# A recommendation tower on one core: the last tile's field pairs in two parts, and first layers one place ahead

## The chip, the cores and the metric

The kernel runs on one core of one Trainium2 chip. The metric is the device time of the program in microseconds (us), as the median of its runs. The profile comes from one execution of its own.

## What is computed

For each of 2048 samples the reference takes 50 rows of 16 numbers, one from each of 50 tables, forms the dot product of every pair of different rows, and runs a small tower of three layers over these 1225 products and 16 dense numbers.

```python
e = jnp.stack([tbl_0[ids[:, 0]], ..., tbl_49[ids[:, 49]]], axis=1)       # 2048 x 50 x 16
gram = jnp.einsum('bid,bjd->bij', e, e)
z = gram[:, I, J]                                                      # the 1225 pairs with i < j
h = jnp.concatenate([z, dense_ctx], axis=1)                            # 1241 columns
h = jnp.maximum(h @ W_top1 + b_top1, 0.0)                              # 512
h = jnp.maximum(h @ W_top2 + b_top2, 0.0)                              # 256
y = h @ W_top3
```

Of the tables 29 have 1000 or 1250 rows (`SMALL`), seven have 12500 and fourteen have 125000.

## The kernel before

**Tiles.** The samples are 16 tiles of 128 (`NTILES`), four to a chunk (`TPC`); `FINAL` is 12, the first tile of the last chunk, and `LAST` is 15. A product of two fp32 numbers is kept exact enough by splitting each into a high and a low fp16 part.

**Where the rows come from.** The 29 small tables and two of 12500 rows (`MED`) lie on the chip: VectorE (DVE) writes one-hot columns (`compare`), TensorE (PE) multiplies them with the table (`look_up`), chunk by chunk and one chunk ahead. ScalarE (ACT) moves the picked rows into `split` (`move`). The other 19 fields (`REST`, `NR` = 19) are gathered from memory by GpSimd (POOL), one indirect DMA for each field and tile (`gathers`, line 448). In the last chunk nothing is looked up any more.

**A tile's way.** When all gathers of a tile have landed, DVE splits them (`split_rows`, lines 576, 580, 589) and transposes all 50 rows in blocks of 32 (`turn`, line 604). PE forms the 50 by 50 products of two samples at a time, a matmul of 32 rows and 100 columns for each of four row groups (`dots`; in the last chunk `half_dots`, line 841, eight halves of 32 matmuls over two row groups and two sample pairs, so 16 matmuls each by the trace's count). ACT and DVE copy each half out of PSUM into `gram` (`copy_half`, lines 1018 and 644); half h waits until half h-2 has been copied. Then nine rectangles (`PIECES`) of `gram` for each of two sides are moved by DMA into `z`, where the pairs i < j lie densely on 125 partitions and 11 columns (`pack`, line 383 on the queue of SyncE, SP). ACT makes the high part of `z` (`split_products`, line 1077), DVE the low part (line 552). The first layer is 33 matmuls of 512 columns (`first_part`, line 881), 22 with the high part and 11 with the low one. The 512 results go through ACT (line 1102), are transposed (`mlp(T, TURN_STEP)`, line 933), copied (line 1106), and multiplied with the second layer's weights (`mlp(T, L2_STEP)`, line 938). DVE makes the last layer (`score`, lines 704 and 706).

**The order.** Every engine runs a list that is written out by hand. Within the last chunk PE has: halves of tile 12 with the first layer of 10 between them; halves of 13; first layers of 11 and 12 with the rest of 11; halves of 14; rest of 12; first layer and rest of 13; halves of 15, from the third on with two matmuls of tile 14's first layer between them (line 902); the rest of 14 (lines 902, 909, 933, 938); and tile 15 (`last_mlp`, lines 854, 858, 866, 874). DVE, ACT and SP have lists to match. All of tile 15's pack follows its last half: SP issues six of side 0, ACT six of side 1 (line 1096), POOL the six small corners (line 472).

**The last tile's gathers.** DVE takes tile 15 in two steps (`last_rows`): the first nine gathered fields with all looked-up ones, then the last ten (lines 620, 624, 625, 636). The halves of tile 15 wait for both.

```python
def half_dots(T, h):
    if h == 0:
        pe.wait_ge(turned_ready, 2 * T + (2 if T < LAST else 4))
```

Of the kernel before, what the change touches and what calls it, by code (L numbers as in the profile page):

```python
# [15 lines left out]
NF = 50  # L16
ND = 16
TILE = 128
TPC = 4
# [25 lines left out]
FIELD = SMALL[:EVEN] + MED + SMALL[EVEN:] + REST  # L45
# [22 lines left out]
JS = EVEN // 2  # L68
JM = NM // 2
# [7 lines left out]
TOP = 5  # L77
PIECES = []
_p = 0
for _g in range(4):  # L80
    _r = ST * _g + TOP + 1
    PIECES.append((_r, NF - _r, ST * _g, ST, _p, 0))
    _p += NF - _r
TOP_P = _p
for _g in range(5):
    PIECES.append((ST * _g + 1, TOP, ST * _g, TOP, TOP_P + TOP * (_g // 2), TOP * (_g % 2)))
DENSE_P = TOP_P + 3 * TOP
DENSE_R = 2
# [66 lines left out]
BIG_PIECES, CORNERS = PIECES[:6], PIECES[6:]  # L155
LAST = NTILES - 1
FINAL = (NCH - 1) * TPC
LAST_KS = (range(0, 6), range(6, ST))
LAST_J = (JS + JM, JS + JM + 5, JJ)
LAST_FIELDS = 2 * (LAST_J[1] - LAST_J[0]) - 1  # L160
HALVES = 2 * EVACS
FILL_FROM, FILL = 2, 2
# [11 lines left out]
ONE_K = ST - 1  # L174
L1_BETWEEN = 6
# [9 lines left out]
def build(nc, small, med, big, ids_small, ids_med, ids_sample, ids_big, dense, w1, w2, b2, w3, y):  # L185
    ctx = ExitStack()
    with ctx:
# [64 lines left out]
        hid_last = gram_ps[:, 0, :]  # L252
# [52 lines left out]
        corners_in = sem("corners_in")  # L305
# [32 lines left out]

        block = ctx.enter_context(nc.Block())
# [5 lines left out]
        def _(sp):  # L345
# [20 lines left out]
            def pack(T, sides=range(TWO), pieces=PIECES):  # L366
# [7 lines left out]

                if T < FINAL:
                    sp.wait_ge(gram_copied, TWO * EVACS * (T + 1))
                else:
                    sp.wait_ge(half_by_act, halves_of(T))
                    sp.wait_ge(half_by_dve, halves_of(T))
                for a in sides:  # L380
                    for piece in pieces:
                        out, src = piece_of(piece, T, a)
                        sp.dma_start(out, src).then_inc(packed[T % 2], 16)  # L383

# [38 lines left out]
            pack(NTILES - 1, (0,), BIG_PIECES)  # L423

        @block.gpsimd
        def _(pool):
# [14 lines left out]
            def gathers(T):  # L441
# [3 lines left out]
                for f in range(NR):  # L445
                    landed = gathered[T % TPC] if T < LAST or f < LAST_FIELDS else gathered_last
                    pace(T, f)
# [21 lines left out]
            for a in range(TWO):  # L469
                for piece in CORNERS:  # L470
                    out, src = piece_of(piece, LAST, a)
                    pool.dma_start(out, src).then_inc(corners_in, 16)

        @block.vector
        def _(dve):
# [89 lines left out]
            def rows_by_parity(T):  # L565

                t = T % TPC
                return [(emb[:, t, 1 - a:NR:2, :], split[:, t, JS + JM + 1 - a:JJ, 0, :, a],
                         split[:, t, JS + JM + 1 - a:JJ, 1, :, a]) for a in range(2)]

            def split_rows(T):
# [10 lines left out]
                known = JS + JM  # L582
# [683 lines left out]
```

## Time and profile before

| what | value |
|---|---|
| runs | 453.38, 453.18 and 456.85 us, median 453.38 us |
| profiled execution, its own time | 453.39 us |
| its span, first to last instruction | 451.3 us |
| mean granted TensorE clock | 0.89 of full speed |
| PE / PE weight loads / DVE / ACT / POOL busy | 76% / 55% / 66% / 44% / 71% |

```profile
POOL 5788777777777777787777777778777777776020
PEclk9978659978679997989999969699998895988999
```

Each digit of these two lines is a fortieth of the span, 11.3 us, in tenths. POOL gathers at an even pace until slice 37 and is then nearly idle. The clock line holds the TensorE clock that was granted: it is full or half in any moment, so a digit between is a mixture.

### The profile page before, as it was taken

How to read it: one execution, taken by the hardware profiler on the slowest of the kernel's cores; microseconds unless marked ns; L12 is line 12 of the kernel's file. 1: busy time of each engine (PE TensorE's matmuls, PEld its weight loads, DVE VectorE, ACT ScalarE, POOL GpSimd, SP SyncE). 2: the span in 40 equal slices, each digit the busy share in tenths (PEclk: the TensorE clock that was granted, in tenths of full speed). 3: DMA queues.
4: the chain of work that ended last, by engine and by line, in shares of the span. 5: the costliest groups of instructions: out<-in, count | busy, mean ns of one | idle time of the engine just before them, and what ended most of it. 6: DMA issues, size and time to landing. Idle time of an engine off the chain costs nothing.

```text
span 451.3 us, 13158 instructions
## 1 busy us (share of the span) xinstructions
PE 342.9 (76%) x5633; PEld 247.4 (55%) x5633; DVE 295.8 (66%) x606; ACT 198.8 (44%) x288; POOL 322.7 (71%) x318
## 2 busy tenths in 40 slices
PE   0568167566488979979989699798895948989886
PEld 0567067565366657666666476656653525454543
DVE  2599899999357579758576687566715437165551
ACT  2335712246235774455457653445487324140511
POOL 5788777777777777787777777778777777776020
PEclk9978659978679997989999969699998895988999
DMA  6994503423321344243213433111121222212020
GB/s 161 407 367 142 173 7 101 118 77 86 82 44 39 104 115 94 63 136 88 47 32 103 115 95 65 36 43 36 40 53 24 66 50 50 48 15 61 5 61 1
DMA packets 24638, 38.92 MB, mean 86 GB/s; under 512 B 8532, under 2 KB 15876, under 8 KB 24452
## 3 DMA queue, kind: packets, MB, share of 16 engines
q1 hardware_dynamic: 14166, 35.04, 24.0%
q0 software_dynamic: 9920, 2.55, 6.6%
q8 instruction: 44, 0.72, 0.7%
q10 hardware_dynamic: 494, 0.49, 0.3%
q14 instruction: 14, 0.11, 0.1%
HBM read 26.98 MB, written 0.14 MB: 60 GB/s over the span
## 4 chain that ended last, share of the span: by engine, by line
PE 34%; DVE 18%; ACT 13%; SPq 11%; issue 10%; DMA 8%; POOL 5%; another core or an unknown queue 0%; DVEq 0%; ACTq 0%; POOLq 0%
PE hid_ps L881 12%; SPq L383 11%; DVE onehot L490 9%; PE look_ps L803 8%; ACT gram L1010 6%; POOL emb L448 5%; DMA ids_bc<-ids_dram 5%; PE mid_ps L938 5%; PE gram_ps L820 3%; ACT z_both L1077 2%; DVE turned L604 2%; PE gram_ps L841 2%; ACT looked L1047 2%; DMA z_both<-gram 2%; DVE w_sb L672 1%
## 5 line engine op out<-in xcount | busy, mean ns | idle before, releaser
L448 POOL DMA_INDIRECT emb<-tbl,gidx x304 | 318.9, 1049 | 95.7 <-issue 88.4
L881 PE MATMUL hid_ps<-w_sb,z_both 127*128 127x512 f16 x462 | 112.3, 386 | 0.0
L803 PE MATMUL look_ps<-parts,onehot 125*128 125x64 f16 x1836 | 75.0, 203 | 44.5 <-DVE onehot L490 29.9
L490 DVE TENSOR_SCALAR onehot<-ids_bc,rows 125x2048 f16<-125x2048 f16 (+1 forms) x144 | 92.2, 690 | 19.2 <-PE look_ps L803 14.7
L803 PEld LDWEIGHTS look_ps<-parts,onehot 125*128 125x128 f16 x1836 | 69.5, 105 | 56.2 <-issue 20.8
L1010 ACT ACTIVATE gram<-gram_ps 50x784 f32<-50x784 f32 x96 | 78.2, 815 | 29.6 <-PE gram_ps L820 26.7
L803 PE MATMUL look_ps<-parts_med,onehot 125*128 125x128 f16 x800 | 57.1, 233 | 14.4 <-DVE onehot L490 13.8
L881 PEld LDWEIGHTS hid_ps<-w_sb,z_both 127*128 127x128 f16 x462 | 41.5, 99 | 46.1 <-issue 3.3
L803 PEld LDWEIGHTS look_ps<-parts_med,onehot 125*128 125x128 f16 x800 | 53.1, 105 | 20.6 <-DVE parts_med L663 13.9
L490 DVE TENSOR_SCALAR onehot<-ids_bc,rows_med 125x1024 f16<-125x1024 f16 x100 | 45.8, 495 | 28.2 <-PE look_ps L803 24.4
L1047 ACT ACTIVATE looked<-look_ps 128x1024 f16<-128x1024 f32 (+1 forms) x28 | 26.7, 954 | 67.0 <-PE look_ps L803 66.6
L820 PE MATMUL gram_ps<-turned 32*128 32x100 f16 x1536 | 28.6, 216 | 25.4 <-ACT gram L1010 23.1
L604 DVE STREAM_TRANSPOSE turned<-split 128x800 uint32<-128x800 uint32 x30 | 46.6, 1625 | 0.5
L938 PE MATMUL mid_ps<-w_sb,h_turned 128*128 128x256 f32 x120 | 37.8, 469 | 2.8 <-ACT h_turned L1106 2.1
L820 PEld LDWEIGHTS gram_ps<-turned 32*128 32x128 f16 x1536 | 20.8, 99 | 31.3 <-ACT gram L1010 25.9
L552 DVE SCALAR_TENSOR_TENSOR z_both<-z_both 127x704 f16<-127x704 f32 x30 | 25.3, 884 | 12.3 <-ACT z_both L1077 12.3
L1102 ACT ACTIVATE h<-hid_ps 128x512 f32<-128x512 f32 x14 | 8.4, 597 | 56.4 <-PE hid_ps L881 51.8
L938 PEld LDWEIGHTS mid_ps<-w_sb,h_turned 128*128 128x128 f32 x120 | 27.2, 238 | 8.5 <-ACT h_turned L1106 2.9
L1077 ACT ACTIVATE z_both<-z_both 127x1408 f16<-127x1408 f32 x15 | 20.6, 1371 | 11.1 <-DMA z_both<-gram 11.1
L644 DVE TENSOR_SCALAR gram<-gram_ps 50x392 f32<-50x392 f32 x32 | 17.4, 568 | 11.7 <-PE gram_ps L841 11.6
L1018 ACT ACTIVATE gram<-gram_ps 50x392 f32<-50x392 f32 x32 | 15.3, 490 | 21.4 <-PE gram_ps L841 21.2
L841 PE MATMUL gram_ps<-turned 32*128 32x100 f16 x512 | 17.4, 223 | 8.8 <-DVE turned L604 5.2
(74 smaller groups left out, 221.7 us busy)
## 6 DMA issues: line engine op xcount, KB each, us to landing
ids_bc<-ids_dram SPq DMA_DIRECT2D x28, 512.0 KB
emb<-tbl,gidx POOLq DMA_INDIRECT x304
z_both<-gram SPq DMA_DIRECT2D x31, 121.0 KB
z_both<-w SPq DMA_DIRECT2D x1, 2816.0 KB
z_both<-gram SPq DMA_DIRECT2D x31, 90.8 KB
z_both<-gram SPq DMA_DIRECT2D x152, 6.2 KB
z_both<-gram SPq DMA_DIRECT2D x31, 60.5 KB
gram<-small SPq DMA_DIRECT2D x2, 512.0 KB, 5.1
```

The costliest lines, as they stand in the source:

```text
L383: sp.dma_start(out, src).then_inc(packed[T % 2], 16)
L448: pool.indirect_dma_start(emb[:, T % TPC, f, :], None, big[f], bass.IndirectOffsetOnAxis(ap=gidx[:, T, f:f + 1], axis=0)).then_inc(landed, 16)
L490: nc.vector.tensor_scalar(onehot[0:TP, s % RING, 0:cnt, :], ids_bc[0:TP, o % IDS_BUFS, 0:cnt, :], row, None, ALU.is_equal).then_inc(onehot ...
L604: nc.vector.transpose(out, src[:, :, w0:w0 + WORDS]).then_inc(turned_ready, 1)
L803: last = nc.tensor.matmul(bank[:, half, at:at + width], onehot[0:TP, at_ring, i, t * TILE:(t + 1) * TILE], moving.rearrange("p i s d -> p ...
L820: last = nc.tensor.matmul(gram_ps[:, r, i * TWO * NF:(i + 1) * TWO * NF], turned[p, T % 2, b:b + TWO, :].rearrange("p a m -> p (a m)"), bu ...
L841: last = nc.tensor.matmul(gram_ps[:, r, i * TWO * NF:(i + 1) * TWO * NF], turned[p, T % 2, b:b + TWO, :].rearrange("p a m -> p (a m)"), bu ...
L881: return nc.tensor.matmul(hid_ps[:, :], z_parts[0:KP, T % 2, x, k, :], w1_sb[0:KP, k, w, :], start=(i == 0), stop=(i == L1_MM - 1))
L938: last = nc.tensor.matmul(out_ps, h1_turned[:, n, :], w2_sb[:, n, :], start=(n == 0), stop=(n == N1 - 1))
L1010: nc.scalar.activation(out, src, ACT.Copy, scale=1.0 / (SCALE * SCALE)).then_inc(gram_copied, 1)
L1047: nc.scalar.activation(out, src, ACT.Copy).then_inc(looked_ready, 1)
L1077: nc.scalar.activation(halves(T, 0), products(T), ACT.Copy, scale=ZSCALE).then_inc(z_hi, 1)
```

## The change

**Order of the fields.** `FIELD` has the 19 gathered fields first (0 to 18), then the odd small one, the other small ones and the two medium ones. The rectangles of `gram` are cut anew: two for the columns 0 to 9 (`LATE_PIECES`), seven for the columns from 10 on (`EARLY_PIECES`), nine in all as before. They hold as many numbers, but in 243 rows of 1280 or 1536 bytes a side, where it was 135 rows of 2816 or 1280 bytes.

**The last tile.** Its gathers run from field 10 to 18 and then 0 to 9. After the first nine, DVE turns fields 10 to 49, PE forms the halves with 80 columns instead of 100, and ACT and DVE copy them (`early_evacuation`, 312 elements instead of 392). Then DVE turns fields 0 to 9, PE forms all pairs with these in `late_dots`, 128 matmuls of 20 columns, ACT and DVE copy them in four pieces each (`late_evacuation`, 160 elements), and the two late pieces a side are packed. The first layer of tile 15 begins with the six columns of `z` that the early pieces fill, and the rest of tile 14 stands between its parts.

**The last chunk.** The first layers of 11, 12 and 13 stand one place ahead: before the halves of 13, after them, and before the halves of 14. The transposes and second layers of 11 and 13 stand between the halves of 13 and 14. The two matmuls of tile 14's first layer between the halves of 15 are gone: it stands as a whole after the late products. In tiles 13 and 14 ACT issues six of side 1's nine pieces, and SP twelve of the eighteen; in tile 15 POOL issues side 1's seven early ones.

```diff
-FIELD = SMALL[:EVEN] + MED + SMALL[EVEN:] + REST
+FIELD = REST + SMALL[EVEN:] + SMALL[:EVEN] + MED
...
+LATE = 10
+LATE_K = 5
+PIECES = [(1, NF - 1, 0, LATE_K, 0, 0), (LATE_K + 1, NF - LATE_K - 1, LATE_K, LATE_K, NF - 1, 0)]
 _p = 0
+for _c in range(LATE, 34, ST - LATE_K):
+    PIECES.append((_c + 1, NF - _c - 1, _c, ST - LATE_K, _p, LATE_K))
+    _p += NF - _c - 1
+_p = sum(nr for _, nr, c, *_ in PIECES if c < LATE)
+for _c in range(34, NF - 1, LATE_K):
+    PIECES.append((_c + 1, NF - _c - 1, _c, LATE_K, _p, 0))
+    _p += NF - _c - 1
+LATE_PIECES, EARLY_PIECES = PIECES[:2], PIECES[2:]
+SP_PIECES, ACT_PIECES = PIECES[:3], PIECES[3:]
...
+LAST_KS = (range(LATE_K, ST), range(LATE_K))
...
 # SyncE
-                for a in sides:
-                    for piece in pieces:
+                for a in range(TWO):
+                    for piece in (PIECES if a == 0 or T <= FINAL else SP_PIECES):
...
+            def pack_last():
+                begin_pack(LAST)
+                sp.wait_ge(half_by_act, halves_of(LAST))
+                sp.wait_ge(half_by_dve, halves_of(LAST))
+                for piece in EARLY_PIECES: ...
+                sp.wait_ge(late_by_act, Q)
+                for piece in LATE_PIECES: ...
...
 # VectorE, the order in the last chunk
             for h in range(HALVES):
                 copy_half(FINAL, h)
+            split_products(FINAL - 1)
+            score(FINAL - 2)
             split_rows(FINAL + 1)
             turn(FINAL + 1)
-            split_products(FINAL - 1)
             for h in range(HALVES):
                 copy_half(FINAL + 1, h)
-            score(FINAL - 2)
+            score(FINAL - 1)
             split_products(FINAL)
-            score(FINAL - 1)
+            split_products(LAST - 2)
             split_rows(LAST - 1)
             turn(LAST - 1)
+            score(FINAL)
             for h in range(HALVES):
                 copy_half(LAST - 1, h)
-            split_products(LAST - 2)
+            score(LAST - 2)
             last_rows(0)
-            score(LAST - 3)
-            last_rows(1)
             for h in range(HALVES):
                 copy_half(LAST, h)
+            last_rows(1)
             split_products(LAST - 1)
-            score(LAST - 2)
+            for r in range(Q):
+                copy_late(r)
+            split_last(0)
             activate(LAST - 1)
+            split_last(1)
             copy_turned(LAST - 1, N1, mlp_copied)
...
 # TensorE
+            def late_dots():
+                T = LAST
+                pe.wait_ge(turned_ready, 2 * T + 4)
+                pe.wait_ge(half_by_act, halves_of(T))
+                pe.wait_ge(half_by_dve, halves_of(T))
+                for h in range(2):
+                    for b in range(0, SPQ, TWO):
+                        for buf in (turned, turned2):
+                            for r in range(Q // 2 * h, Q // 2 * (h + 1)):
+                                p = slice(32 * r, 32 * r + 32)
+                                last = nc.tensor.matmul(
+                                    gram_ps[:, r, b * LATE:(b + TWO) * LATE],
+                                    turned[p, T % 2, b:b + TWO, :].rearrange("p a m -> p (a m)"),
+                                    buf[p, T % 2, b:b + TWO, 0:LATE], start=(buf is turned), stop=(buf is turned2))
+                    last.then_inc(late_done, 1)
...
+            first_part(FINAL - 1, 0, L1_MM)
             for h in range(HALVES):
                 half_dots(FINAL + 1, h)
-            first_part(FINAL - 1, 0, L1_MM)
-            mlp(FINAL - 1, TURN_STEP)
-            first_part(FINAL, 0, L1_BETWEEN)
-            mlp(FINAL - 1, L2_STEP)
-            first_part(FINAL, L1_BETWEEN, L1_MM)
+                if h == TURN_AT:
+                    mlp(FINAL - 1, TURN_STEP)
+                if h == L2_AT:
+                    mlp(FINAL - 1, L2_STEP)
+            high_part(FINAL)
+            low_part(FINAL)
+            mlp(FINAL, TURN_STEP)
+            mlp(FINAL, L2_STEP)
+            high_part(LAST - 2)
+            low_part(LAST - 2)
             for h in range(HALVES):
                 half_dots(LAST - 1, h)
-            mlp(FINAL, TURN_STEP)
-            mlp(FINAL, L2_STEP)
-            first_part(LAST - 2, 0, L1_MM)
-            mlp(LAST - 2, TURN_STEP)
-            mlp(LAST - 2, L2_STEP)
-            fill = 0
+                if h == TURN_AT:
+                    mlp(LAST - 2, TURN_STEP)
+                if h == L2_AT:
+                    mlp(LAST - 2, L2_STEP)
             for h in range(HALVES):
                 half_dots(LAST, h)
-                if h >= FILL_FROM:
-                    high_part(LAST - 1, fill, fill + FILL)
-                    fill += FILL
-            high_part(LAST - 1, fill, 2 * ST)
+            late_dots()
+            high_part(LAST - 1)
             low_part(LAST - 1)
+            last_high(0)
+            last_low(0)
             mlp(LAST - 1, TURN_STEP)
+            last_high(1)
             mlp(LAST - 1, L2_STEP)
+            last_low(1)
             last_mlp()
...
 # ScalarE
+            copy_mlp(FINAL - 1, FEED - 1)
             for h in range(HALVES):
                 copy_half(FINAL + 1, h)
+                if h == TURN_AT:
+                    copy_mlp(FINAL - 1, TURN_STEP + 1)
             split_products(FINAL)
-            copy_mlp(FINAL - 1, FEED - 1)
-            copy_mlp(FINAL - 1, TURN_STEP + 1)
+            pack(FINAL + 1)
             copy_mlp(FINAL, FEED - 1)
-            for h in range(HALVES):
-                copy_half(LAST - 1, h)
             copy_mlp(FINAL, TURN_STEP + 1)
             split_products(LAST - 2)
             copy_mlp(LAST - 2, FEED - 1)
-            copy_mlp(LAST - 2, TURN_STEP + 1)
-            split_products(LAST - 1)
+            for h in range(HALVES):
+                copy_half(LAST - 1, h)
+                if h == TURN_AT:
+                    copy_mlp(LAST - 2, TURN_STEP + 1)
+            pack(LAST - 1)
             for h in range(HALVES):
                 copy_half(LAST, h)
-            pack(LAST, BIG_PIECES)
+            split_products(LAST - 1)
+            for r in range(Q):
+                copy_late(r)
+            pack_late()
```

`high_part(T)` and `low_part(T)` are now the 22 and the 11 matmuls of a first layer; the first waits for the high part of `z` alone.

## Rows read from the trace of the kernel before

**Rows 1.** Chain that ended last, from tile 13's last gather: start us, us, what.

```profile
366.11 2.40 DMA emb<-tbl,gidx
...
379.68 8.94 PE hid_ps L881 x33
...
443.31 1.09 PE gram_ps L858 x5
...
449.18 0.27 ACT h L1194
```

**Rows 2.** Timeline, gathers: start us, us, engine, line; in brackets the idle time before.

```profile
402.24 0.95 POOL L448 DMA_INDIRECT emb<-tbl,gidx  x1 [0.30 <-issue]
...
415.04 0.95 POOL L448 DMA_INDIRECT emb<-tbl,gidx  x1 [0.30 <-issue]
...
417.30 0.32 DVE L620 TENSOR_SCALAR split<-emb 128x80 f16<-128x80 f32 x2 [4.65 <-DMA emb<-tbl,gidx]
```

**Rows 3.** Timeline, what ends second layer 10 and starts first layer 11.

```profile
365.42 1.37 ACT L1077 ACTIVATE z_both<-z_both 127x1408 f16<-127x1408 f32 x1
365.57 1.99 PE L938 MATMUL mid_ps<-w_sb,h_turned 128*128 128x256 f32 x8 [0.69 <-ACT h_turned L1106]
...
372.56 1.67 DVE L552 SCALAR_TENSOR_TENSOR z_both<-z_both 127x704 f16<-127x704 f32 x2
```

**Rows 4.** Timeline, halves of products: tile 13 at half clock, tile 14 at full.

```profile
374.98 1.33 PE L841 MATMUL gram_ps<-turned 32*128 32x100 f16 x32 [1.05 <-DVE gram L644]
...
376.58 1.33 PE L841 MATMUL gram_ps<-turned 32*128 32x100 f16 x32 [0.28 <-ACT gram L1018]
...
400.15 1.01 PE L841 MATMUL gram_ps<-turned 32*128 32x100 f16 x32 [0.63 <-DVE gram L644]
400.72 1.05 DVE L644 TENSOR_SCALAR gram<-gram_ps 50x392 f32<-50x392 f32 x2 [0.23 <-PE gram_ps L841]
```

**Rows 5.** Timeline, weight loads of products: over four row groups, then over two.

```profile
346.86 0.64 PEld L820 LDWEIGHTS gram_ps<-turned 32*128 32x128 f16 x32 [3.92 <-ACT gram L1010]
...
351.35 0.63 PEld L841 LDWEIGHTS gram_ps<-turned 32*128 32x128 f16 x16 [0.65 <-issue]
...
423.40 0.38 PEld L841 LDWEIGHTS gram_ps<-turned 32*128 32x128 f16 x16 [0.42 <-issue]
```

**Rows 6.** Windows of one microsecond: PE, PEld, DVE, ACT, POOL busy, PEclk, DMA, GB/s.

```profile
373.00:374.00 1.00, 0.93 (x32) 0.70 (x26) 1.00 (x2) 0.30 (x1) 0.69 (x2) 0.50 0.28 65
...
382.00:383.00 1.00, 1.00 (x4) 0.30 (x3) 1.00 (x2) 0.00 (x0) 1.00 (x1) 0.50 0.51 147
...
402.00:403.00 1.00, 0.73 (x29) 0.61 (x30) 1.00 (x2) 0.97 (x2) 0.76 (x1) 1.00 0.15 24
...
404.00:405.00 1.00, 0.82 (x4) 0.41 (x2) 0.38 (x1) 0.45 (x2) 0.70 (x2) 0.50 0.04 3
...
410.00:411.00 1.00, 1.00 (x5) 0.40 (x4) 1.00 (x2) 0.00 (x0) 0.95 (x1) 0.80 0.11 15
```

**Rows 7.** Timeline, the rest of a tile: transposes, second layer at half clock, score.

```profile
417.80 0.63 PE L933 MATMUL mid_ps<-identity,h 128*128 128x128 f32 x4 [0.78 <-ACT h L1102]
418.47 0.60 ACT L1106 ACTIVATE h_turned<-mid_ps 128x512 f32<-128x512 f32 x1 [0.81 <-PE mid_ps L933]
...
405.50 3.78 PE L938 MATMUL mid_ps<-w_sb,h_turned 128*128 128x256 f32 x8 [0.69 <-ACT h_turned L1106]
```

**Rows 8.** Timeline, last tile's turning on DVE, and the packs' issue on each queue.

```profile
409.23 2.50 DVE L636 STREAM_TRANSPOSE turned<-split 128x640 uint32<-128x640 uint32 x2
...
404.46 13.44 SPq L383 DMA_DIRECT2D z_both<-gram  x18
...
428.63 5.60 ACTq L1096 DMA_DIRECT2D z_both<-gram  x6
429.17 3.06 POOL L472 DMA_DIRECT2D z_both<-gram  x6 [13.19 <-DVE gram L644]
...
435.49 1.47 ACT L1087 ACTIVATE z_both<-z_both 127x768 f16<-127x768 f32 x2 [7.05 <-DMA z_both<-gram]
```

More of the change, by code:

```diff
@@ L364, in load_sample_ids, with begin_pack @@
                 sp.dma_start(odd[:, n % 2, :, :], ids_sample[n, :, :, :]).then_inc(sample_in[n % 2], 16)
-            def pack(T, sides=range(TWO), pieces=PIECES):
+            def begin_pack(T):
                 if T >= 2:
@@ L373, in pack @@
                              dense[:, T, :, :]).then_inc(dense_in[T % 2], 16)
+            def pack(T):
+                begin_pack(T)
                 if T < FINAL:
@@ L422, in _ @@
                     pack(T - 1)
-            pack(NTILES - 1, (0,), BIG_PIECES)
+            pack_last()
         @block.gpsimd
@@ L444, in gathers @@
                     pool.wait_ge(emb_read, T + 1 - TPC)
-                for f in range(NR):
-                    landed = gathered[T % TPC] if T < LAST or f < LAST_FIELDS else gathered_last
-                    pace(T, f)
+                for i in range(NR):
+                    f = (LATE + i) % NR
+                    landed = gathered[T % TPC] if T < LAST or f >= LATE else gathered_last
+                    pace(T, i)
                     pool.indirect_dma_start(
@@ L468, in _ @@
             pool.wait_ge(half_by_dve, halves_of(LAST))
[L469 to L472, printed above, removed]
+            for piece in EARLY_PIECES:
+                out, src = piece_of(piece, LAST, 1)
+                pool.dma_start(out, src).then_inc(early_by_pool, 16)
         @block.vector
@@ L567, in rows_by_parity @@
                 t = T % TPC
-                return [(emb[:, t, 1 - a:NR:2, :], split[:, t, JS + JM + 1 - a:JJ, 0, :, a],
-                         split[:, t, JS + JM + 1 - a:JJ, 1, :, a]) for a in range(2)]
+                return [(emb[:, t, a:NR:2, :], split[:, t, 0:JR - a, 0, :, a], split[:, t, 0:JR - a, 1, :, a])
+                        for a in range(2)]
             def split_rows(T):
@@ new lines, in last_high, with last_low @@
+            def last_high(i):
+                T = LAST
+                pe.wait_ge(z_hi, T + 1 + i)
+                for k in LAST_KS[i]:
+                    for w in range(2):
+                        nc.tensor.matmul(hid_last, z_parts[0:KP, T % 2, 0, k, :], w1_sb[0:KP, k, w, :],
+                                         start=(i == 0 and k == LAST_KS[0][0] and w == 0), stop=False)
+            def last_low(i):
+                T = LAST
+                pe.wait_ge(z_split, T + 1 + i)
+                for k in LAST_KS[i]:
+                    last = nc.tensor.matmul(hid_last, z_parts[0:KP, T % 2, 1, k, :], w1_sb[0:KP, k, 0, :],
+                                            start=False, stop=(i == 1 and k == LAST_KS[1][-1]))
+                if i == 1:
+                    last.then_inc(mlp_done, 1)
@@ L860, in last_mlp @@
-                last.then_inc(mlp_done, 1)
                 pe.wait_ge(scored, T)
@@ L1093, in pack, with pack_late @@
                 act.wait_ge(half_by_dve, halves_of(T))
-                for piece in pieces:
+                for piece in ACT_PIECES:
                     out, src = piece_of(piece, T, 1)
                     act.dma_start(out, src).then_inc(packed[T % 2], 16)
+            def pack_late():
+                act.wait_ge(z_split, LAST - 1)
+                act.wait_ge(late_by_dve, Q)
+                for piece in LATE_PIECES:
+                    out, src = piece_of(piece, LAST, 1)
+                    act.dma_start(out, src).then_inc(late_in, 16)
             def copy_mlp(T, g):
```

141 lines of the change are left out of this document (75 added, 66 removed).

## The prediction

> **What bounds the kernel now.** I read the page's slices first: POOL gathers evenly to slice 37 of 40. Then the chain of waits: until 366 us it follows the gathers, and from tile 13's last gather on it is nearly all PE, with first layers back to back [rows 1]. Only the order after 366 us is changed in what it waits for; ahead of that SP's eighteen issues a tile (13.4 us [rows 8]) fit between gathers, and no gather is added, so I take everything up to 367.6 us, the end of tile 10's second layer [rows 3], as it was. The last gather starts at 415.0 and DVE has it at 417.3, 2.3 us later; the ninth one of tile 15 starts at 402.2, so its data are there at about 404.5 [rows 2]. That is 12.8 us in hand for the early pairs. The third view is the timeline, for durations, and the fourth the windows, for the clock. The first layer of tile 15 ends at 444.4, and 6.9 us follow to the span's end, 451.3 [rows 1]; the profiled execution took 453.39, so 2.1 lie around the span, and it equals the median of 453.38.
>
> **The new chain, step by step.** Matmuls of 512 columns take 0.217 us each at full clock (5 in 1.09 [rows 1]), so a first layer costs 7.15.
>
> (1) Tile 11's high part ends at 366.8; DVE's low part (1.7 [rows 3]) now comes at once, so the layer runs from 368.7 to 375.8, in what was a hole of PE. Low part and score ahead of tile 13's rows make its turning 0.9 late (373.6), behind that layer.
>
> (2) Halves of 13. A pair of halves is paced by DVE's copy: 1.28 at full clock, 1.60 and 1.77 at half (starts 400.15 to 401.44; 374.98 to 376.58 and on [rows 4]). The transposes (0.64) and second layer 11 (1.99) now stand between. PE: 2 halves 0.97, 0.64, 2 halves 0.97, 1.99, 2 halves 0.97, a pair that waits 1.3: 6.9, to 382.7; copies to 383.3.
>
> (3) ACT makes tile 12's high part after its copies: 1.37, to 384.7. First layer 12: 7.15, to 391.9. A fall of the clock here (below) adds 1.2: 393.1.
>
> (4) Transposes and second layer 12: 0.61 + 0.17, 0.64, 0.60 + 0.17, 1.99 [rows 3, 7], together 4.2: 397.3.
>
> (5) Tile 13's pack: SP's twelve issues at 0.75 (13.44 / 18 [rows 8]) from 383.3 give 392.3, with about 2 to land 394.3; ACT's six (5.60 [rows 8]) run from 384.7 to 390.3, before it has to copy layer 12. High part to 395.7, low to 397.4: just hidden by step 4. First layer 13: 404.5.
>
> (6) Tile 14's turning waits for that low part on DVE: rows 1.2, transposes 3.1, score 0.9, done 402.6, hidden. Halves of 14 with the rest of 13 between: 6.9, to 411.4; copies 412.0.
>
> (7) DVE: score 0.93, split 0.87, transposes 2.50 [rows 8], 0.14 to PE: 416.4. PE is idle for 5 us, since tile 14 is only being packed (SP 412.0 to 421.0, plus 2; high part by 424.4). The early data have waited since 404.5: the 12.8 us in hand are lost here.
>
> (8) Eight early halves. The copies shrink from 0.58 to 0.49: between ACT's 784 and 392 elements the step is about 0.8 ns an element, DVE's 0.57 for 392 leaves 0.16 fixed. At full clock 4.3, at half 6.4 by the pitch of tile 13; less columns take off some, I take 5.6: 422.0, copies 422.5.
>
> (9) Fields 0 to 9 need all early halves read: split 0.92, transposes 0.76, 0.14: 424.4. Gathers landed at 417.3, so POOL is off the chain.
>
> (10) `late_dots`, 128 matmuls and weight loads of a size that the trace does not show. Nearest rows: 20 ns each over four row groups even at half clock, 39 at half clock and 24 at full over two [rows 5]. So 2.6 to 5.0 us; the columns are a fifth, the weight loads as before; I take 27 ns, 3.4: 427.8.
>
> (11) First layer 14 whole, 7.15, plus 2.35 for the clock: 437.3. Beside it lie, hidden: late copies (4 of 0.3 on ACT and DVE, by 428.6), two late DMAs a queue (1.5 to 1.9 and about 2 to land, 432.5), SP's seven early ones (5.2) and POOL's seven (0.51 each [rows 8]), both parts of `z` to 435. If that cover went, 2 to 3 us of packing would show.
>
> (12) 18 matmuls 3.9, transposes 0.64, 10 matmuls 2.2, second layer 1.99, 5 matmuls 1.1: 9.8, to 447.1. (13) The end as before, 6.9: span 454.0, time **456.1 us**, 2.7 above the 453.4 of the profiled execution and of the median.
>
> In the same points first layer 14 ended at 433.0 before and 11.4 followed; filling the waits of tile 14's rest gives back 1.6, and steps 7 to 11 take more.
>
> **Smaller edits.** More rows per DMA: issue is 0.75 on average for pieces of 5 and of 44 rows alike [rows 8], so nothing, up to 0.1 a piece (1.2 a pack, hidden in step 11, half open in step 5). Two longer memsets at the start and the moved gather order: 0 to 0.3, beside work that POOL's pace covers. ACT's issuing in tile 14 runs 412.0 to 417.6, so its first early copy is up to 0.6 late, inside step 8.
>
> **The clock.** The granted clock fell from 2.4 to 1.2 GHz by 373, after PE had idled since 367.6, and stayed down through all halves of 13 and over 3 us of dense matmuls, to past 383; it fell again by 404 after five microseconds of halves alone, in which PE was 73% busy, and rose only at 410.4, five after dense work resumed [rows 6]. The first cost 1.8 (8.94 for 7.15 [rows 1]); the second made a second layer 3.78 instead of 1.99 [rows 7]. The halves with dense work between them (tile 15's, before) kept it up. Here steps 6 to 10 are halves, 5 us idle, halves, idle, late products: down. Dense time at half clock loses half: 1.7 to 3.4 in step 11, I take 2.35, and 0 to 3.4 in step 3 (halves and 2 us idle), I take 1.2.
>
> The Trainium skill (TensorE: Matmul & The Clock Gate, "What's actually happening") says that the default is throttled and that activity releases it, by how busy the PE has recently been. By busyness alone late products and halves would hold the clock up and the sum would be the first rival's; the windows of tile 14's halves speak against that.
>
> **Rivals.**
> A. The clock holds. Against: both falls above. For: dense work lies inside the halves of 13 and 14. Then step 3 loses 1.2, step 8 1.3, step 10 about 0.6 and step 11 2.35 less: 5.4 off, 450.7; range 448 to 453.4.
> B. Slower: the clock falls already inside the halves of 13, behind their first pairs. Place: steps 2, 3 and 11. Price: step 3 takes its 3.4 (2.2 more), step 11 its 3.4 (1.0 more), late products 39 ns (1.6 more): 460.9, less if one part stays away; 457.9 to 462. It decides once the clock is down when first layer 12 starts and again for over half of first layer 14.
> C. The split does what its wording says: early pairs finish before the last gather. For: 12.8 us in hand. Against: DVE's list and step 7; even the clock at full brings the early halves only to about 419. A gain over 1% would need this with A, about 447.
>
> **How the numbers follow.** Likeliest (454 to 458.5) 0.45; A 0.24, B 0.28, C 0.03. One per cent, which is about what a measurement can tell from no change, is 4.5: faster is below 448.9, slower above 457.9. Faster: C and 0.08 of A, 0.11. Slower: B and 0.08 of the likeliest, 0.36. Between: 0.53. The bounds of the unknown steps give 450.2 (steps 3, 8, 10, 11 low: 1.2, 1.3, 0.8, 2.35 and 0.3) to 461.8 (2.2, 0.8, 1.6, 1.05); 450 to 460.5 leaves out about two in ten.
>
> **What would show it.** First layer 11 starting at 368.7 (step 1); halves of 13 lasting 7 with a second layer inside (2); first layer 13 done by 404.5 and ACT's six issues between (5); PE idle for 5 us ahead of early halves that begin near 416 (7); late products of 2.6 to 5.0 (10); a granted clock of 0.50 at the start of first layer 14, and that layer at 9.5 instead of 7.15 (11); 9.8 from its end to that of tile 15's (12). Wrong makes it: a clock of 1.00 there, early halves before 412, or a first layer 13 or 14 that waits for its pack.

## The result, and the profile after

The changed kernel takes 461.03 us as the median of four executions (459.06 to 463.04), beside 454.04 us for the kernel before on the same chip: ratio 1.0151, 95% interval [1.0118, 1.0184]. It is slower by 7 us, where 456.1 was forecast. Its profiled execution took 463.04, with a span of 461.2, and a second one 460.71, with a span of 458.9. Here and below medians are of all executions, and ratios leave out those that took over 1.5% more than the fastest of the same kernel.

The page of the kernel before gives, for the chain that ended last, by engine:

```profile
PE 34%; DVE 18%; ACT 13%; SPq 11%; issue 10%; DMA 8%; POOL 5%; another core or an unknown queue 0%; DVEq 0%; ACTq 0%; POOLq 0%
```

The same line of the page of the changed kernel:

```profile
PE 32%; SPq 23%; DVE 18%; ACT 10%; DMA 10%; issue 7%; DVEq 0%; ACTq 0%
```

The share of SP's queue has doubled and POOL is gone from the chain. (Such shares scatter: a second profile of the kernel before, shown below, has SP's queue at 3% and POOL at 39%; one of the changed kernel has SP's again at 23%.) So the place to look is ahead of the last chunk. On the timeline of the kernel before, two packs on SP (18 DMAs each) and ACT's high part between them:

```profile
329.29 13.41 SPq L383 DMA_DIRECT2D z_both<-gram  x18
343.88 1.38 ACT L1077 ACTIVATE z_both<-z_both 127x1408 f16<-127x1408 f32 x1 [1.14 <-DMA z_both<-gram]
349.46 13.40 SPq L383 DMA_DIRECT2D z_both<-gram  x18
```

The same packs, with the high parts of tiles 10 and 11, in the changed kernel:

```profile
336.94 13.91 SPq L407 DMA_DIRECT2D z_both<-gram  x18
352.01 1.38 ACT L1163 ACTIVATE z_both<-z_both 127x1408 f16<-127x1408 f32 x1 [1.64 <-DMA z_both<-gram]
357.59 13.91 SPq L407 DMA_DIRECT2D z_both<-gram  x18
373.89 1.37 ACT L1163 ACTIVATE z_both<-z_both 127x1408 f16<-127x1408 f32 x1
```

The pack takes 0.5 us longer to issue and starts 7.7 us later; the next one 8.1. It did not start so: the second pack of the kernel starts at 128.01 before and at 128.03 after, the fifth at 197.04 and 201.75, the eighth at 264.46 and 271.86. Meanwhile gathers keep their pace (the last one at 416.76, [rows 2] had 415.04). The changed kernel's chain of waits shows why a pack is late (start us, us, what):

```profile
336.10 0.83 ACT gram L1089
336.93 0.02 issue
336.94 0.74 SPq L407
...
341.60 0.79 SPq L407
...
343.20 0.70 SPq L407
...
349.39 0.72 SPq L407
...
350.15 1.84 DMA z_both<-gram
...
352.01 1.38 ACT z_both L1163
353.39 0.71 ACT gram L1089
```

The rows show a loop: from the last copy by ACT (336.10) through eighteen issues to the next copy (353.39). A pack's eighteen issues, its landing (1.84), ACT's high part, ACT's copies of the next tile's products, which stand behind it in ACT's list; and only when they are done may SP begin the next pack. One turn took 20.17 us before (329.29 to 349.46) and 20.65 here, and two thirds of it are issue on SP. The landing is not what grew: the pack at 309.31 in the kernel before landed 1.83 us after its last issue. The kernel before has the loop as well; its page had SP at 11% of the chain, and the prediction passed over it.

Behind the steady part, the timeline of the changed kernel on PE, for the steps of the prediction:

```profile
374.05 1.99 PE L1011 MATMUL mid_ps<-w_sb,h_turned 128*128 128x256 f32 x8 [0.69 <-ACT h_turned L1202]
377.05 7.30 PE L955 MATMUL hid_ps<-w_sb,z_both 127*128 127x512 f16 x33 [1.00 <-DVE z_both L589]
...
392.97 7.75 PE L975 MATMUL hid_ps<-w_sb,z_both 127*128 127x512 f16 x22 [1.85 <-ACT z_both L1163]
...
407.02 4.91 PE L975 MATMUL hid_ps<-w_sb,z_both 127*128 127x512 f16 x22
...
425.61 0.97 PE L889 MATMUL gram_ps<-turned 32*128 32x80 f16 x32 [4.84 <-DVE turned L675]
...
433.24 1.81 PE L907 MATMUL gram_ps<-turned 32*128 32x20 f16 x128 [2.29 <-DVE turned L675]
434.98 7.24 PE L975 MATMUL hid_ps<-w_sb,z_both 127*128 127x512 f16 x22
...
444.43 2.75 PE L919 MATMUL look_ps<-w_sb,z_both 127*128 127x512 f16 x12
```

The second layer of tile 10 starts 8.5 us later than in [rows 3]; from its start to the span's end are 87.2 us, where the kernel before had 85.7. Two of its windows of a microsecond show the clock at half where first layer 12 and first layer 14 run:

```profile
397.00:398.00 1.00, 1.00 (x3) 0.30 (x2) 0.00 (x0) 0.00 (x0) 0.70 (x2) 0.50 0.25 57
...
435.00:436.00 1.00, 1.00 (x7) 0.41 (x4) 0.97 (x4) 0.49 (x2) 0.71 (x2) 0.50 0.30 85
```

### The profile page after: what moved, and what is told of

The parts are those of the page before. It is cut to its first block, busy times and chain, and to the rows that moved or that the text cites. A ratio compares the mean times of both kernels' runs of the same rounds, so it can differ in the third digit from the quotient of the medians.

```text
span 461.2 us, 13426 instructions
## 1 busy us (share of the span) xinstructions
PE 343.6 (74%) x5761; PEld 248.1 (54%) x5761; DVE 296.6 (64%) x610; ACT 199.0 (43%) x292; POOL 325.7 (71%) x319
## 4 chain that ended last, share of the span: by engine, by line
PE 32%; SPq 23%; DVE 18%; ACT 10%; DMA 10%; issue 7%; DVEq 0%; ACTq 0%
SPq L407 22%; DVE onehot L527 8%; PE hid_ps L955 8%; PE look_ps L850 6%; DMA ids_bc<-ids_dram 5%; ACT gram L1089 5%; PE hid_ps L975 4%; PE mid_ps L1011 4%; DMA z_both<-gram 4%; ACT z_both L1163 3%; PE gram_ps L889 3%; PE gram_ps L867 2%; PE hid_ps L982 2%; DVE turned L640 1%; DVE w_sb L717 1%
## 5 line engine op out<-in xcount | busy, mean ns | idle before, releaser
L955 PE MATMUL hid_ps<-w_sb,z_both 127*128 127x512 f16 x396 | 95.6, 381 | 1.0 <-DVE z_both L589 1.0
L850 PE MATMUL look_ps<-parts_med,onehot 125*128 125x128 f16 x800 | 56.7, 232 | 14.4 <-DVE onehot L527 13.9
L955 PEld LDWEIGHTS hid_ps<-w_sb,z_both 127*128 127x128 f16 x396 | 34.4, 98 | 37.9 <-DVE z_both L589 1.4
L867 PE MATMUL gram_ps<-turned 32*128 32x100 f16 x1536 | 28.2, 215 | 32.1 <-ACT gram L1089 29.9
L683 DVE TENSOR_SCALAR gram<-gram_ps 50x392 f32<-50x392 f32 (+1 forms) x32 | 16.7, 546 | 15.0 <-PE gram_ps L889 14.5
L1097 ACT ACTIVATE gram<-gram_ps 50x392 f32<-50x392 f32 (+1 forms) x32 | 14.5, 473 | 18.6 <-PE gram_ps L889 18.1
L1151 ACT ACTIVATE split<-looked 128x256 f16<-128x256 f16 (+1 forms) x60 | 21.5, 428 | 0.1
```

Of the source, the lines that this page charges most:

```text
L850: last = nc.tensor.matmul(bank[:, half, at:at + width], onehot[0:TP, at_ring, i, t * TILE:(t + 1) * TILE], moving.rearrange("p i s d -> p ...
L867: last = nc.tensor.matmul(gram_ps[:, r, i * TWO * NF:(i + 1) * TWO * NF], turned[p, T % 2, b:b + TWO, :].rearrange("p a m -> p (a m)"), bu ...
L955: return nc.tensor.matmul(hid_ps[:, :], z_parts[0:KP, T % 2, x, k, :], w1_sb[0:KP, k, w, :], start=(i == 0), stop=(i == L1_MM - 1))
```

## The experiments

"L2(10)" is the start of tile 10's second layer in the profiled execution, and "the tail" is what lies from there to the span's end. Ratios are to the kernel before, timed on the same chip in the same rounds.

**The new cut alone, in the old order.**

```diff
-PIECES of the kernel before (rows 44, 33, 22, 11 and five of 5)
+PIECES of the changed kernel (rows 49, 44, 39, 33, 27, 21, 15, 10, 5)
-DENSE_R = 2
+DENSE_R = 4
-ONE_K = ST - 1
+ONE_K = DENSE_K
```

> The kernel before with the new cut of the rectangles alone (same nine pieces a side, 243 rows instead of 135), old order of fields, old gathers, old last chunk. Theory 1 (the loop of the steady part: a pack's issue and landing, ACT's high part, ACT's copies of the next tile, next pack; the new cut lengthens it): the twelve packs start later one by one, tile 10's second layer starts 6 to 9 us later (at 372 to 375), and the time is 455 to 459 us, since the last chunk of the kernel before has about 5 us of PE idle ahead of tile 13's halves to absorb it. Theory 2 (order of fields and of gathers slows the steady part): 453 to 455, second layer 10 near 366. Theory 3 (the new order of the last chunk alone is slow): the same 453 to 455.

Measured: 453.28 us, ratio 0.9969 [0.9937, 1.0001]. A pack's issue is 13.91, L2(10) is at 371.83, where the theory had it; the time is not up, and there the theory missed. Its PE timeline shows where the lateness went:

```profile
371.83 1.99 PE L941 MATMUL mid_ps<-w_sb,h_turned 128*128 128x256 f32 x8 [0.69 <-ACT h_turned L1109]
373.76 0.72 PE L844 MATMUL gram_ps<-turned 32*128 32x100 f16 x32
```

Set beside it the first halves of tile 13 in the kernel before:

```profile
372.78 1.15 PE L841 MATMUL gram_ps<-turned 32*128 32x100 f16 x32 [5.21 <-DVE turned L604]
```

In the old order PE stands idle for 5.21 us ahead of these halves, because they wait for tile 13's gathers [rows 1]. A second layer that comes 6.3 us later fills that idle time, and the halves start only one microsecond later (373.76 for 372.78), after which the clock is down for a shorter while (3.4 us instead of 10.2). The tail is 79.0 us instead of 85.7. So the cut's price was paid, and taken back by a wait.

**The kernel before, once more.** 

> The kernel before, unchanged, looked at once more, to see how far the start of second layer 10 scatters between profiled executions: if by less than 1 us from 365.6, the 2.2 us that e2 is late there are part of the change (order of fields or of gathers); if by 2 or more, they are scatter.

Measured: 453.13 us, span 451.0. L2(10) is at 368.05, so one kernel scatters by 2.5 us there, and the idle time ahead of the halves of 13 shrinks to match, in this execution's timeline:

```profile
368.05 1.99 PE L938 MATMUL mid_ps<-w_sb,h_turned 128*128 128x256 f32 x8 [0.69 <-ACT h_turned L1106]
373.23 1.17 PE L841 MATMUL gram_ps<-turned 32*128 32x100 f16 x32 [3.19 <-DVE turned L604]
```

With L2(10) at 365.6, 368.1 and (new cut) 371.8 the old order ends at 451.3, 451.0 and 450.8. The chain that ended last, by engine, looks quite different from that of the first profile, though the kernel and its span are the same:

```profile
POOL 39%; PE 21%; issue 14%; DVE 13%; DMA 8%; SPq 3%; ACT 3%; DVEq 0%; POOLq 0%; ACTq 0%
```

Gathers and packs run beside each other at nearly the same pace, and either can be what the end is followed back to.

**The change with the old cut.** `LATE_PIECES` are the old rectangles that hold the pairs with fields 0 to 9, the early ones the other seven; tile 15's first layer waits for all of them.

```diff
-PIECES of the changed kernel
+PIECES of the kernel before
+LATE_PIECES = [PIECES[0], PIECES[4]]
+EARLY_PIECES = PIECES[1:4] + PIECES[5:]
-LAST_KS = (range(LATE_K, ST), range(LATE_K))
+LAST_KS = (range(0, 6), range(6, ST))
```

> The changed kernel with the old cut: 135 rows a side; the late pieces of the last tile are the first large one and the first corner, and its first layer waits for all pieces. Theory 1: second layer 10 back at 365 to 367 and the whole at 451.5 to 455 us. Theories 2 and 3: it stays at 459 to 462; under theory 2 second layer 10 is still near 374, under theory 3 it is near 366 and the loss is behind it.

Measured: 454.83 us, ratio 0.9991 [0.995, 1.0031]; pack 13.40, L2(10) 367.75, span 453.2, tail 85.5. Everything of the change but the cut is here, and nothing is lost or won. Its second layer 10 and first layer 12:

```profile
367.75 1.99 PE L1013 MATMUL mid_ps<-w_sb,h_turned 128*128 128x256 f32 x8 [0.69 <-ACT h_turned L1203]
...
386.34 6.61 PE L977 MATMUL hid_ps<-w_sb,z_both 127*128 127x512 f16 x22 [1.85 <-ACT z_both L1165]
```

Its idle time ahead of the early halves is 4.91, its late products again take 1.81.

**The changed kernel with a shorter pack.** Tiles 0 to 14 leave out the smallest rectangle, ten of each sample's products, so a pack has 16 issues.

```diff
-SP_PIECES, ACT_PIECES = PIECES[:3], PIECES[3:]
+MOST = PIECES[:-1]
+SP_PIECES, ACT_PIECES = MOST[:3], MOST[3:]
```

> The changed kernel without its smallest rectangle (5 rows of 5 columns, the last nine fields' corner) in the packs of tiles 0 to 14: two DMAs less a pack, 16 instead of 18, 1.4 us less of issue a tile; ten products of each side's samples are left out there. Everything else as changed. If the packs' issue in the steady part is the cause: second layer 10 starts 8 to 14 us earlier than 374 (until the gathers set the pace), and the time falls to 449 to 455 us. If the loss lies in the last chunk: 459 or more.

Measured: 455.41 us, ratio 1.0014 [0.9978, 1.0051], 5.6 below the changed kernel (up to 455 was expected). The profiled execution was the fastest of the ten (450.96; the slowest took 459.33), and two packs with the high part between them stand so:

```profile
327.92 12.45 SPq L408 DMA_DIRECT2D z_both<-gram  x16
341.59 1.38 ACT L1164 ACTIVATE z_both<-z_both 127x1408 f16<-127x1408 f32 x1 [0.22 <-DMA z_both<-gram]
347.07 12.45 SPq L408 DMA_DIRECT2D z_both<-gram  x16
...
362.39 1.99 PE L1012 MATMUL mid_ps<-w_sb,h_turned 128*128 128x256 f32 x8 [0.69 <-ACT h_turned L1203]
```

A turn of the loop takes 19.15 us, L2(10) is at 362.39, and the tail is 86.8, near that of the changed kernel, with 1.17 us in it for which the halves of 13 wait for gathers again. This carries the verdict: the order and the split are untouched, two issues a pack are gone (in tiles 13 and 14 one of SP's and one of ACT's), and the time comes back.

**A longer pack, before's order and cut.** The largest rectangle as two of 22 rows: 20 issues (in the last tile one more on SP and one more on ACT).

```diff
+PIECES[0:1] = [(TOP + 1, 22, 0, ST, 0, 0), (TOP + 23, 22, 0, ST, 22, 0)]
```

> The kernel before with its largest rectangle of each side moved as two of 22 rows: same rows and bytes, two more DMAs in every pack, 20 instead of 18, so 1.4 to 1.5 us more of issue per tile and nothing else. Theory 1: the packs start later by up to 1.5 us a tile, second layer 10 at 375 to 382, time 460 to 468 us. Theories 2 and 3: 453 to 455.

Measured: 466.21 us, ratio 1.0234 [1.0171, 1.0297], as expected, with the same bytes in the same rows. Tile 10's high part, 343.88 in the kernel before, and its second layer:

```profile
360.29 1.38 ACT L1078 ACTIVATE z_both<-z_both 127x1408 f16<-127x1408 f32 x1 [1.40 <-DMA z_both<-gram]
...
382.00 1.99 PE L939 MATMUL mid_ps<-w_sb,h_turned 128*128 128x256 f32 x8 [0.69 <-ACT h_turned L1107]
```

L2(10) is 14 us late, more than the old order's idle time covers, and so the time is up. Over issue times of 12.45, 13.40, 13.91 and 14.96 a pack, L2(10) is at 362.4, at 367.6 (mean of eight executions of kernels with the old cut, 364.7 to 370.4), at 372.6 (three with the new cut, 371.8 to 374.1) and at 382.0. The last turn of the loop, from tile 10's pack to tile 11's, less the issue of the pack is 6.70, 6.76, 6.74 and 6.86 us in the traces shown: the turn is the issue and a constant. The 362.4 is from the fastest of ten executions; its kernel's median would have it near 366.8 (an estimate: 455.41 less the 1.8 us between time and span and the tail of 86.8), hardly ahead of the old cut. There the chain that ended last has POOL at 16% and SP's queue at 5%, so there gathers rather than packs set the pace, and a still shorter pack would have little left to give.

**The changed kernel, once more.** 

> The changed kernel once more, for the scatter of its steady part. The theory (the new cut's issue on SP lengthens each turn of the loop of packs): the second layer of tile 10 starts at 371 to 375 us again (changed kernel 374.1, kernel before with the new cut alone 371.8), with eighteen issues of a pack at 13.8 to 14.0, and the time is 458 to 463. The rival (the late start was one execution's accident, and the spread of 365.6 to 370.4 seen with the old cut is what both cuts have): it starts below 370.

Measured: 460.71 us, span 458.9; pack 13.91, L2(10) 371.88, tail 87.0:

```profile
371.88 1.99 PE L1011 MATMUL mid_ps<-w_sb,h_turned 128*128 128x256 f32 x8 [0.69 <-ACT h_turned L1202]
```

The late start is the cut's, not one execution's.

**Breaking the loop.** The kernel before with ACT's high part behind the copies of the next tile, so that a pack need not wait for it.

> The kernel before with ACT's high part of tile T-2 after, instead of before, its copies of the second half of tile T-1 (and DVE's low part at the end of its slot): the pack of a tile no longer waits for the landing of the one before. Theory 1: packs start earlier, second layer 10 at 364 or earlier, time 448 to 453 us. Theories 2 and 3 say that no such loop bounds: within 1 us of before, or slower because the first layers get their halves later.

Measured: 464.01 us, ratio 1.0173 [1.0101, 1.0245]. The expectation missed by more than 10 us. In its profiled execution, the slowest of four (471.99), SP's queue is down to 3% of the chain that ended last and PE up to 53%: the loop is broken, and a slower chain through first layers and look-ups has taken its place, with L2(10) at 389.12. The high part now comes later than the first layer and the next use of `z` want it; that this is the whole cost was not separated.

**The new order with the last tile whole.** First layers of 11 to 13 one place ahead and ACT's share of the packs, but fields, cut and tile 15 as before.

```diff
+            first_part(FINAL - 1, 0, L1_MM)
             for h in range(HALVES):
                 half_dots(FINAL + 1, h)
-            first_part(FINAL - 1, 0, L1_MM)
...
+            pack(LAST - 1, PIECES[3:])
             split_products(LAST - 1)
             for h in range(HALVES):
                 copy_half(LAST, h)
```

> The kernel before with the new order of the last chunk up to tile 14 (first layers 11, 12 and 13 one place ahead, rest of 11 and 13 inside the halves of 13 and 14, ACT issuing six pieces in tiles 13 and 14), but old cut and last tile whole, as before: no late products. The cut theory with its corollary (the new order has no idle time ahead of tile 13 and runs as one chain of PE from second layer 10 on): second layer 10 at 365 to 368, halves of 14 end near 412 instead of 404, halves of 15 begin 422 to 424 instead of 421, time 453 to 458 us. The rival, that the order is a gain and only the split of the last tile loses: below 452 us.

Measured: 466.65 us, ratio 1.0285 [1.0239, 1.0332]; L2(10) 370.39, tail 95.0. The expectation, at most 458, missed by more than 8 us. Halves of tile 15 in its timeline:

```profile
422.57 1.17 PE L841 MATMUL gram_ps<-turned 32*128 32x100 f16 x32 [6.45 <-DVE turned L636]
429.38 0.85 PE L841 MATMUL gram_ps<-turned 32*128 32x100 f16 x16 [5.64 <-ACT gram L1023]
```

Moving the first layers ahead leaves PE with nothing but the last tile, which waits for turning (6.45), and then for ACT, whose high part of tile 14 stands ahead of its copies and waits for the pack (5.64). The split last tile and that high part behind the copies, which the change with the old cut has and this run has not, together make the new order no dearer than the old one; they were not tried apart.

**Holding the clock.** The change with the old cut, and matmuls whose result nobody reads in PE's waits (20 ahead of tile 15's early halves, one per pair of them, and eight behind).

```diff
+            hold_clock(20)
             for h in range(HALVES):
                 half_dots(LAST, h)
+                if h % 2 == 1:
+                    hold_clock(1)
+            hold_clock(8)
             late_dots()
```

> The changed kernel with the old cut (as e2), and 32 matmuls of 512 columns on constant operands, whose results nobody reads, where PE idles: 20 ahead of the early halves, one after every pair of them, 8 ahead of the late products. Theory: the idle time there lets the clock fall to 1.2 GHz, and it is down for 17 us into first layer 14; with the fill it stays at 2.4 and first layer 14 takes 7.2 instead of 8.9 to 9.6, the early halves 4.9 instead of 5.4: 1.5 to 3 us less than e2. Rival, that the halves' pitch and waits are set by DVE and ACT alone and the first layer by its data: no change, or 1 us more, since the fill delays the halves.

Measured: 454.04 us, ratio 0.9995 [0.9942, 1.0048]; tail 84.1, 1.4 less than without, and in the time no difference that can be told from none. The clock is at full from 393.5 on; its windows over the early halves and the late products:

```profile
420.00:425.00 5.00, 4.36 (x133) 3.15 (x134) 3.61 (x9) 3.01 (x8) 0.00 (x0) 1.00 0.13 38
427.00:430.00 3.00, 2.06 (x130) 1.82 (x131) 1.93 (x3) 1.65 (x4) 2.46 (x6) 1.00 0.49 133
```

First layer 14 then takes 7.1 us instead of 8.9, but its start, measured from L2(10), is 0.6 later (60.1 for 59.5): PE had been waiting for DVE and ACT, and the late products took longer, not shorter (they stretch over 2.8 us, with 0.93 in which nothing is issued).

**The same for the kernel before.** One such matmul per pair of halves of tile 14.

> The kernel before with one filling matmul of 512 columns after every pair of halves of tile 14, nothing else. If the fall of the clock at 403 to 410 there comes of the halves' thin work: second layer 12 takes 1.99 instead of 3.78 and first layer 13 7.2 instead of 7.8, the halves of 15 begin 1.5 to 2.5 us earlier (then the last gather sets them), time 451.5 to 453.5 us. If the clock's fall has no price, because something else ends the wait: no change.

Measured: 453.75 us, ratio 0.999 [0.9968, 1.0012], no measurable gain. Second layer 12 takes 1.99 instead of 3.78 [rows 7], and the next rows show the gain lost twice:

```profile
410.79 7.29 PE L887 MATMUL hid_ps<-w_sb,z_both 127*128 127x512 f16 x33 [1.00 <-DVE z_both L552]
...
436.32 3.32 PE L944 MATMUL mid_ps<-w_sb,h_turned 128*128 128x256 f32 x8 [0.78 <-DVE h_turned L655]
```

First layer 13 waits for its low part, and the clock falls later instead, at 437, in second layer 14.

**Two attempts at a better kernel.** Old cut, the old order up to first layer 13, then early halves with the rest of 13 between them and the late products. The first has filling matmuls ahead of tile 13's halves and after each pair in 13 and 14. The second has ACT's high part of 13 earlier, DVE's first step for fields 0 to 9 ahead, and the filling in tile 14, in the last early halves and ahead of the late products.

> Old cut and old order up to first layer 13 (so idle time ahead of tile 13 takes up a late second layer 10, and tile 14's halves run as soon as its gathers have landed), and then the new end: early halves of tile 15 with the rest of 13 inside, late products, first layer 14, tile 15 in between; 12 filling matmuls ahead of tile 13's halves and one after every pair in 13 and 14. If the loss of the new last chunk is its serial order and its gain the split of the last tile: early halves begin at 412 to 415, late products at 419 to 422, and the time is 446 to 450 us. If the split gains nothing: 452 to 455.

> e7 with its own waits mended: ACT makes tile 13's high part ahead of its copies of 14, first layer 13 starts on the high part alone, DVE splits the last ten fields while second layer 13 runs and only transposes them after the early halves, filling matmuls stand between the last early halves and ahead of the late products, and none ahead of tile 13's. First layer 13 1 us earlier, late products 1 to 2 us earlier, first layer 14 at 7.3 instead of 9.7 if the clock stays at 2.4 GHz: 449 to 452 us, 0.5 to 1 per cent less than before. If the clock falls in spite of the filling: 452 to 454.

Measured: 454.59 us, ratio 1.0026 [0.9984, 1.0067], and 454.35 us, ratio 1.0025 [0.9993, 1.0057]. Both missed. The second one's late products and first layer 14, with the clock over the latter:

```profile
421.35 1.62 PE L921 MATMUL gram_ps<-turned 32*128 32x20 f16 x122 [0.21 <-DVE turned L687]
424.60 0.25 PE L921 MATMUL gram_ps<-turned 32*128 32x20 f16 x6 [1.63 <-issue]
424.78 6.49 PE L995 MATMUL hid_ps<-w_sb,z_both 127*128 127x512 f16 x22
```

```profile
424.00:426.00 2.00, 1.40 (x9) 0.58 (x10) 1.05 (x5) 0.48 (x2) 0.68 (x2) 0.64 0.13 33
426.00:428.00 2.00, 2.00 (x6) 0.76 (x5) 0.39 (x2) 0.00 (x0) 0.00 (x0) 0.50 0.31 89
```

The late products begin four microseconds earlier than in the change with the old cut, but within them PE issues nothing for 1.63 us, and first layer 14 follows only 2.5 us earlier, its first matmuls at half clock in spite of the filling. No version beats the kernel before by what can be measured.

## Why the prediction was wrong, and where it was right

**The step that failed is the opening one:** "ahead of that SP's eighteen issues a tile (13.4 us ...) fit between gathers ... so I take everything up to 367.6 us ... as it was", and with it, under the smaller edits, more rows per DMA costed at "nothing, up to 0.1 a piece". The size was inside that bound (13.91 for 13.40 is 0.03 a piece), though its ground was an average: in the old cut rectangles of 11 to 44 rows take 0.73 to 0.80 us and those of 5 rows 0.67 to 0.69. The cover was not there. I looked for SP's work against POOL's gathers, with which it never competes, and not against what waits for SP. Ahead of tile 10's second layer there are eleven packs. The changed kernel's chain of waits runs through eight of them (not the third, seventh and tenth, where it follows look-ups and first layers on PE), and eight times 0.51 is 4.1; L2(10) moved by 5.0 between the means. From pack to pack the means of the three and the eight executions differ by -0.5 to 1.2 us, so the 0.5 holds for the sum and for the last turn, not for every turn. That the chain of waits followed gathers until 366 was true only of its end, from 336 on: SP's 11% on the page lay farther ahead.

A smaller part is not the cut's: the profile that the forecast started from has L2(10) at 365.6, 2.0 ahead of the mean of the eight executions. The old order hides such a difference, and the new one does not. The mean start with the new cut is thus 7.0 later than the forecast's, and the tail gave 1.2 back.

**Why the lateness counted here and not with the cut alone.** In the old order the halves of 13 wait for gathers, and up to about 6 us of a late loop vanish in that wait (the new cut alone, and the kernel before once more: span 451 whatever L2(10)). In the new one first layer 11 stands in that hole and starts when pack 11 has come (377.05, 1.00 idle for the low part), so that the kernels with it and the split last tile end 85.5 to 87.2 us after L2(10): 453.2, 449.2, 458.9 and 461.2 for starts of 367.75, 362.39, 371.88 and 374.05 (84.1 with the clock held, 95.0 with the last tile whole). The cut alone costs nothing, the rest alone costs nothing, and the two together cost 7 us: neither part's time tells that of the sum.

**The tail, step by step, was 88.4 us in the forecast's terms and 87.2 in the trace,** 1.2 the other way. All places below are later than forecast by the 8.5 us.
- Steps 1 and 2: first layer 11 at 377.05 (forecast with the shift 377.2), halves of 13 done at 391.1 (391.2). Right.
- Step 3: the clock fell where it was doubted; first layer 12 took 10.1 instead of the 8.4 forecast. Its price was 2.8, of the 0 to 3.4 considered.
- Steps 4 to 6: second layer 12, first layer 13 and halves of 14 end at 420.8, 17.7 us after first layer 12 (18.3). Pack 13 came in time.
- Step 7: idle 4.84 (5). Steps 8 and 9: 7.6 from early halves to late products (8.0).
- Step 10: the term most in error, 1.81 us instead of 3.4 and below the lower bound of 2.6. A hundred and twenty-eight matmuls with their weight loads, over two row groups at a time, take 14 ns each at half clock. [rows 5] has 39 over two row groups, with 100 columns, and 20 over four, which I had taken as the floor. The step let only the columns shrink and kept the weight loads as they were; no row showed that, and with a fifth of the columns the time fell to about a third. In the Trainium skill (TensorE: Matmul & The Clock Gate, "Wait — 56ns, not 53.3ns?") starts are never closer than about 25 ns however few the columns; over two row groups the trace has 14, so the measurement decides.
- Step 11: 9.45 for 9.5. Step 12: 9.5 for 9.8. The end: 7.3 for 6.9.
- In the paragraph on the clock, PE was 73% busy in one microsecond, 402 to 403; over the five, 398 to 403, it was 77%.

**The rivals.** A (the clock holds, 5.4 off) was not what happened, and was overpriced: with the clock held by filling behind tile 14 only 1.4 came back, in one execution each. B's 460.9 is next to the 461.0 measured, but for another reason: the clock was at full in the halves of 13, first layer 14 lost 2.4 and not 3.4, and the late products gained. Only its first condition, the clock down when first layer 12 starts, held, and cost 1.6 more than the 1.2 that the forecast had; the second, half clock for over half of first layer 14, was just missed (4.7 of 9.5 us). C did not happen: the early halves began at 425.6, nine microseconds after the last gather's start, with DVE's list and the 4.84 us of idle time as step 7 had it.

**Not settled:** why L2(10) scatters by some 6 us between executions with the same issue time (in the eight with the old cut the third and the seventh turn each differ by up to 1.8 us, and the fifth and the tenth are some 2 us longer in one or two), and what else than a late high part made the attempt to break the loop dear.

## What to carry to other kernels

Before a part of a kernel is taken as it was, follow one full turn of its steady state and ask what each engine's list waits for from the others; a queue that is idle a third of the time can still be the longest link of a loop, and then each tenth of a microsecond comes back in every turn that it bounds. A wait that an order has in it is slack for whatever runs late ahead of it: an edit that fills it makes every earlier lateness count, so two edits that are free by themselves need to be tried together. And a stall of PE whose cause is another engine gives little back by keeping the clock up.

## What the runs showed of the hardware

The time that SP needs to issue one DMA of this kind goes neither with its bytes nor simply with its rows. In the chain of the changed kernel the nine rectangles of 49, 44, 39, 33, 27, 21, 15, 10 and 5 rows take 0.74, 0.75, 0.76, 0.74, 0.71, 0.71, 0.79, 0.72 and 0.70 us, and the largest number is the one with 15 rows. In the kernel before, rectangles of 33, 22 and 11 rows take 0.74, 0.73 and 0.73 us, and those of 5 rows less (here 22 rows and 5 rows):

```profile
310.92 0.73 SPq L383
...
313.21 0.67 SPq L383
```

The Trainium skill (DMA: Bandwidth & Descriptors, "Why a DMA increments its semaphore by 16 and not by 1") says that a DMA is spread over the largest number of engines up to 16 that divides the slowest dimension of both sides, here the rows: 7, 11, 13, 11, 9, 7, 15, 10 and 5 in the new cut, and 11 for each of 44, 33, 22 and 11 rows in the old one. The issue times rise in that order but for the first of the pack, which suggests that a rectangle is cheap to issue if its count of rows has a small such divisor. The times repeat from pack to pack, but no run tried this by itself.

The same page says (in "Issuing engines are not separate DMA queues") that the time to initiate a DMA is usually small relative to the DMA itself; here one takes some 0.75 us to initiate and 1.84 us from there to land, and with eighteen in one list it is 13.9 against 1.84, so the trace disagrees for many small transfers.

The small matmuls of the late products keep nearly the same pace at either clock: 14 ns each at half clock (128 in 1.81 us), 13 at full clock (100 in 1.34 us with the clock held, 122 in 1.62 us in the second attempt). In both runs with filling matmuls there PE then issued nothing for a while (0.93 and 1.63 us); what paused it was not found.
